# A linear-attention block and a ternary feed-forward on one Trainium2 core: the last block's output in two halves, and 32 row matmuls in three pieces

## What is computed

```python
q, k, v = x@Wq.T + bq, x@Wk.T + bk, x@Wv.T + bv        # 16 heads of 16 channels
q = softmax(q, axis=-1); k = softmax(k, axis=-2)        # k over the tokens
state = einsum('bhnd,bhne->bhde', k, v)
out   = einsum('bhnd,bhde->bhne', q, state)
x = layernorm(x + (layernorm(out)*ln_g + ln_b) @ Wo.T + bo)
h = layernorm(x)*ln1_g + ln1_b
h = gelu(h @ ternary(w1).T + b1)                        # 256 -> 1024
y = (layernorm(h)*ln2_g + ln2_b) @ ternary(w2).T + b2   # 1024 -> 256
x = layernorm(x + y)
```

## Time and profile before

| what | value |
|---|---|
| median of 3 runs | 592.26 us (591.04 to 594.32) |
| profiled execution, its own time | 591.67 us |
| its span, first to last instruction | 589.9 us |
| mean granted TensorE clock | 0.985 |
| busy share: PE, DVE, ACT, POOL | 93%, 86%, 82%, 68% |
| chain that ended last, by engine | PE 56%, POOL 14%, ACT 11%, DVE 10%, issue 5%, DMA 2% |

### The profile page before, as it was taken

How to read it: one execution, slowest core, us unless ns; L and a number is a source line. 1 busy time by engine, 2 the same in 40 slices (tenths; PEclk the granted TensorE clock), 3 DMA queues, 4 the chain that set the end, 5 groups by cost and what they waited for, 6 DMA issues and landing times.

```text
span 589.9 us, 10943 instructions
## 1 busy us (share of the span) xinstructions
PE 549.4 (93%) x3584; PEld 498.6 (85%) x3584; DVE 507.2 (86%) x1294; ACT 480.8 (82%) x938; POOL 398.3 (68%) x384
## 2 busy tenths in 40 slices
PE   1989999999999999999699999999999999999990
PEld 1879999999889999988679888888988888889890
DVE  3998888787979878866767999999999999999985
ACT  4461779787868978775979999999999999999983
POOL 0463779769597876658647876667678766765672
PEclk9999999999999999989999999999999999999996
DMA  5632013060613203052010022211212222010002
GB/s 161 266 118 73 1 73 144 0 215 2 221 66 134 83 11 135 1 181 107 37 71 2 2 107 73 72 36 38 73 72 73 71 75 66 34 45 37 37 37 107
DMA packets 11256, 46.53 MB, mean 79 GB/s; under 512 B 1344, under 2 KB 1728, under 8 KB 9024
## 3 DMA queue, kind: packets, MB, share of 16 engines
q1 hardware_dynamic: 11200, 45.83, 21.6%
HBM read 29.02 MB, written 16.81 MB: 78 GB/s over the span
## 4 chain that ended last, share of the span: by engine, by line
PE 56%; POOL 14%; ACT 11%; DVE 10%; issue 5%; DMA 2%; POOLq 0%; SPq 0%; ACTq 0%; DVEq 0%
PE ring L1727 18%; PE qps_sps_aps_then_y L1751 18%; PE qps_sps_aps_then_y L1600 5%; PE qps_sps_aps_then_y L1617 4%; POOL xt L401 3%; POOL xc_lo L380 3%; POOL xt_lo L390 3%; ACT z L677 2%; ACT zjunk L669 2%; PE ring L1540 2%; PE qps_sps_aps_then_y L1522 2%; PE ring L1669 2%; POOL qw L411 2%; DVE z L1092 1%; ACT ring L720 1%
## 5 line engine op out<-in xcount | busy, mean ns | idle before, releaser
L1751 PE MATMUL qps_sps_aps_then_y<-ff_w_over_xc_lo,ff_a_lo_over_qw 128*128 128x258 f32 x512 | 126.3, 283 | 0.0
L1751 PE MATMUL qps_sps_aps_then_y<-ff_w_over_xc_lo,ff_a_hi_over_xc_lo 128*128 128x258 f32 x512 | 126.2, 283 | 0.0
L1727 PE MATMUL ring<-ff_ht_hi_over_qw,t 128*128 128x512 f32 x256 | 106.1, 414 | 3.0 <-DVE ff_sums L1218 1.1
L1727 PE MATMUL ring<-ff_ht_lo_over_xc_hi,t 128*128 128x512 f32 x256 | 101.2, 395 | 0.0
L1751 PEld LDWEIGHTS qps_sps_aps_then_y<-ff_w_over_xc_lo,ff_a_hi_over_xc_lo 128*128 128x128 f32 x512 | 96.9, 189 | 3.5
L1751 PEld LDWEIGHTS qps_sps_aps_then_y<-ff_w_over_xc_lo,ff_a_lo_over_qw 128*128 128x128 f32 x512 | 96.6, 189 | 3.4
L1179 DVE SCALAR_TENSOR_TENSOR ff_a_lo_over_qw<-ring,ff_rho,ff_a_hi_over_xc_lo 128x512 fp32r<-128x512 f32 x128 | 91.5, 741 | 7.9 <-ACT ff_a_hi_over_xc_lo L738 6.9
L720 ACT ACTIVATE ring<-ring,bias 128x512 f32<-128x512 f32 x128 | 84.1, 675 | 11.8 <-PE ring L1727 10.5
L493 POOL TENSOR_TENSOR ff_accp_over_xt_lo<-ff_accp_over_xt_lo,ff_sq_over_ek_et_hi 128x512 f32<-128x512 f32 x64 | 84.0, 1313 | 11.4 <-ACT ff_sq_over_ek_et_hi L736 7.0
L736 ACT ACTIVATE ff_sq_over_ek_et_hi<-ring 128x512 f32<-128x512 f32 x128 | 78.7, 615 | 0.5
L738 ACT CAST ff_a_hi_over_xc_lo<-ring 128x512 fp32r<-128x512 f32 x128 | 77.5, 605 | 0.0
(11 more groups left out here) (175 smaller groups left out, 1673.0 us busy)
## 6 DMA issues: line engine op xcount, KB each, us to landing
x_scratch<-z SPq DMA_DIRECT2D x16, 514.0 KB, 3.0
ff_x_over_w_raw_xc<-x_scratch SPq DMA_DIRECT2D x16, 514.0 KB, 4.7
xt<-in_x_tok_dram SPq DMA_DIRECT2D x8, 1024.0 KB, 4.8
out_dram<-ff_z_over_et_lo SPq DMA_DIRECT2D x16, 512.0 KB, 3.5
xc<-in_x_chan_dram SPq DMA_DIRECT2D x7, 1024.0 KB, 6.9
w_raw<-in_w_dram SPq DMA_DIRECT2D x2, 1024.0 KB, 6.5
xc<-in_x_chan_dram SPq DMA_DIRECT2D x2, 512.0 KB, 6.8
rows<-in_rows_dram SPq DMA_DIRECT2D x1, 384.0 KB, 6.5
```

What stands on the lines that cost most here:

```text
L1727: mm = nc.tensor.matmul(ff_bank(k, m), t1[:, c, m * P:(m + 1) * P], h[:, k % 2, c], start=(c == 0 and j == 0), stop=(c == CH - 1 and j == 1))
L1751: last = nc.tensor.matmul(ff_yps[:, t, 0:C + 2], a[:, m % DEPTH, t * P:(t + 1) * P], ff_w2[:, m], start=(m == 0 and j == 0), stop=(m == FC ...
```

## The change

Three edits.

1. `ternary_rows` takes a range. 8 of the 32 matmuls stay at their place, 16 go between `state_product(7)` and `state_transpose(7)`, 8 between `state_transpose(7)` and `ff_first(0,0)`. `folded_rows` moves in DVE's list from before `k_maximum(7,1)` to behind `projected_low(7)`, and POOL's `ff_keep_residual(0, .)` gets a wait for it (`f_out` at 3).
2. On DVE `ff_hidden_stats(15)`, which leads to the block's first variance (the hidden one), goes ahead of `ff_centre_y(15, .)`. The last iterations of DVE's loop are written out.
3. Block 15 gets small tiles of its own (`l_mv`, `l_ve`, `l_rs`, `l_shift`) and goes in halves of two token tiles: variance, power, shift for each half. ACT scales tiles 0, 1 and 2, DVE tile 3, and SP stores two halves of 256 KB.

```diff
 (SP)
             ff_store(NK - 2)
-            ff_store(NK - 1)
-            for par in range(2):
-                sp.wait_ge(ff_o_out[par], 8 * NK)
+            for g in range(2):
+                sp.wait_ge(l_act, g + 2)
+                if g == 1:
+                    sp.wait_ge(l_dve, 1)
+                sp.dma_start(out[NB - 1, :, T - TB + 2 * g:T - TB + 2 * g + 2], ff_z[:, (NK - 1) % 2, 2 * g:2 * g + 2]
+                             ).then_inc(ff_o_out[(NK - 1) % 2], 16)
+            sp.wait_ge(ff_o_out[0], 8 * NK)
+            sp.wait_ge(ff_o_out[1], 8 * NK + 16)
 (POOL, ff_keep_residual and the end of its list)
                 if k == 0:
                     pool.wait_ge(xe_mm, NB)
+                    pool.wait_ge(f_out, 3)
...
-            for k in range(4, NK + 4):
+            for k in range(4, NK + 3):
...
+            for g in range(2):
+                pool.wait_ge(l_eps, g + 1)
+                nc.gpsimd.tensor_tensor(l_rs[:, 2 * g:2 * g + 2], l_ve[:, 2 * g:2 * g + 2], nhalf[:, 0:2], ALU.pow
+                                        ).then_inc(l_rstd, 1)
 (ACT)
-            for k in range(3, NK + 3):
+            for k in range(3, NK + 2):
...
+            for n in range(3):
+                act.wait_ge(l_nmr, n // 2 + 1)
+                nc.scalar.activation(ff_z[:, (NK - 1) % 2, n], ff_z[:, (NK - 1) % 2, n], ACT.Identity,
+                                     bias=l_shift[:, n:n + 1], scale=l_rs[:, n:n + 1]).then_inc(l_act, 1)
 (DVE)
+            def last_variance(g):
+                ts = slice(2 * g, 2 * g + 2)
+                dve.wait_ge(ff_z_stat, TB * (NK - 1) + 2 * g + 2)
+                nc.vector.memset(fence[:], 0.0)
+                for n in range(2 * g, 2 * g + 2):
+                    nc.vector.bn_aggr(l_mv[:, n], ff_bnZ[:, n]).then_inc(ff_z_var, 1)
+                dve.wait_ge(ff_z_var, TB * (NK - 1) + 2 * g + 2)
+                nc.vector.tensor_scalar(l_ve[:, ts], l_mv[:, ts, 1], EPS, None, ALU.add).then_inc(l_eps, 1)
+
+            def last_shift(g):
+                ts = slice(2 * g, 2 * g + 2)
+                dve.wait_ge(l_rstd, g + 1)
+                nc.vector.scalar_tensor_tensor(out=l_shift[:, ts], in0=l_mv[:, ts, 0], scalar=-1.0, in1=l_rs[:, ts],
+                                               op0=ALU.mult, op1=ALU.mult).then_inc(l_nmr, 1)
...
-            folded_rows()
             k_maximum(NB - 1, 1)
...
             projected_low(NB - 1)
+            folded_rows()
             product_stats(NB - 1, 0)
...
+            ff_residual(NK - 2, (2, 3))
+            ff_hidden_mean(NK - 1)
+            ff_hidden_stats(NK - 1)
+            ff_centre_y(NK - 1, (0, 1))
+            ff_centre_y(NK - 1, (2, 3))
+            ff_out_stats(NK - 2, (2, 3))
+            ff_out_variance(NK - 2)
+            ff_residual_gain(NK - 1)
+            ff_residual(NK - 1, (0, 1))
+            ff_out_stats(NK - 1, (0, 1))
+            ff_out_shift(NK - 2)
+            last_variance(0)
+            ff_residual(NK - 1, (2, 3))
+            ff_out_stats(NK - 1, (2, 3))
+            last_variance(1)
+            last_shift(0)
+            last_shift(1)
+            dve.wait_ge(l_nmr, 2)
+            nc.vector.tensor_scalar(ff_z[:, (NK - 1) % 2, 3], ff_z[:, (NK - 1) % 2, 3], l_rs[:, 3:4], l_shift[:, 3:4],
+                                    ALU.mult, ALU.add).then_inc(l_dve, 1)
 (PE)
-            def ternary_rows():
-                pe.wait_ge(f_tern, 8)
-                pe.wait_ge(f_bsum, 1)
...
+            def ternary_rows(first, last):
+                if first == 0:
+                    pe.wait_ge(f_tern, 8)
+                    pe.wait_ge(f_bsum, 1)
+                for n in range(first, last):
...
-            ternary_rows()
+            ternary_rows(0, 4)
             attend(NB - 2, 0)
...
             state_product(NB - 1)
+            ternary_rows(4, 12)
             state_transpose(NB - 1)
+            ternary_rows(12, 16)
             ff_first(0, 0)
             state_project(NB - 1)
```

More of the change, by code:

```diff
@@ L165, in both_halves @@
         ff_gain = sb("ff_gain", [P, TB])
+        l_ve, l_rs, l_shift = sb("l_ve", [P, TB]), sb("l_rs", [P, TB]), sb("l_shift", [P, TB])
+        l_mv = sb("l_mv", [P, TB, 2])
         early = ExitStack()
@@ L250, in both_halves @@
             sem(s) for s in ("ff_yc_ok", "ff_z_ok", "ff_z_stat", "ff_z_var", "ff_z_eps", "ff_z_rstd", "ff_z_nmr", "ff_o_ok"))
+        l_eps, l_rstd, l_nmr, l_act, l_dve = (sem(s) for s in ("l_eps", "l_rstd", "l_nmr", "l_act", "l_dve"))
         ff_o_out = [sem(f"ff_o_out{n}") for n in range(2)]
@@ L1432, in _ @@
             ff_hidden_stats(0)
-            for k in range(1, NK + 2):
+            for k in range(1, NK - 1):
                 ff_norm_apply(k + 2, (0, 1))
@@ L1458, in _ @@
                 ff_hidden_stats(k)
+            ff_out_stats(NK - 3, (2, 3))
+            ff_act_low(NK - 1, 3)
+            ff_act_low(NK - 1, 4)
+            ff_out_variance(NK - 3)
+            ff_residual_gain(NK - 2)
+            ff_act_low(NK - 1, 5)
+            ff_residual(NK - 2, (0, 1))
+            ff_out_stats(NK - 2, (0, 1))
+            ff_act_low(NK - 1, 6)
+            ff_act_low(NK - 1, 7)
+            ff_square_sum(NK - 1, 7)
+            ff_out_shift(NK - 3)
+            ff_square_total(NK - 1)
+            ff_residual(NK - 2, (2, 3))
[18 more added lines that the diff above has]
+                                    ALU.mult, ALU.add).then_inc(l_dve, 1)
         @block.tensor
@@ L1490, in ternary_bias @@
                 last.then_inc(f_bias, 1)
-            def ternary_rows():
-                pe.wait_ge(f_tern, 8)
-                pe.wait_ge(f_bsum, 1)
[L1495 to L1503, removed]
+            def ternary_rows(first, last):
[3 more added lines that the diff above has]
+                for n in range(first, last):
+                    h, m = n // FC, n % FC
+                    for piece in range(2):
+                        j = VEC[("ln2_g", "ln2_b")[h]][0] + m
+                        mm = nc.tensor.matmul(
+                            qps[:, h * C:(h + 1) * C], vparts[:, j, piece:piece + 1].to_broadcast([P, P]),
+                            t2[:, m], start=(n == 0 and piece == 0),
+                            stop=(m == FC - 1 and piece == 1), skip_group_check=True)
+                if last == 2 * FC:
+                    mm.then_inc(f_rows, 1)
             def q_product(b, v):
```

## The result

The changed kernel takes **586.74 us** (median of 4 runs, 586.42 to 587.22); the kernel before took 591.95 us beside it (4 runs, 591.04 to 594.32). The ratio is 0.989, with a 95% interval of 0.987 to 0.991: 5.2 us faster. The forecast was 585.4 us.

The account below looks back on a forecast made before the run. PE bounds the feed-forward blocks, row matmuls the path near 261 us, a serial tail the end. Terms -4.0 - 0.65 - 0.7 - 0.9 - 0.6 = -6.9 us: profiled 584.8, forecast 585.4 against median 592.26; range 583.4 to 588.3.

Parts of the forecast that it names:

- First place, -4.0: Around 261 us, 24 of 32 row matmuls leave (3.04 us) and PE's 0.99 us wait goes: -4.0 us, other end 2.5.
- POOL's lateness: At the change of stage, POOL's ff_rs late by some 0.5 us, absorbed; rival that POOL limits the gain to 2.5: chance 0.11.
- Second place, 0: Change of stage: 2.9 us of moved matmuls meet 4.0 us of PE idle time, so 0 us.
- Clock -0.65: state_project(7): filled PE gaps keep the clock at its upper level, 1.66 us becomes 1.01: -0.65 us, ends 0 and 0.65.
- port -0.7: r_lo of batch 7: a new wait holds POOL's ff_x1c behind it, 1.69 us becomes 0.96: -0.7 us, ends 0 and 0.73.
- End, scalings -0.9: Last block in halves: tile 2 scaled at 585.8 to 585.9 instead of 586.79, -0.9 us including +0.2 for hidden variance first.
- Store -0.6: Last store: the last 256 KB needs half of the 1.28 us transfer of 512 KB, -0.6 us, ends 0 and half of 1.28.
- the forecast's own sign of being wrong: At the end: a last store that lands 2.6 us after issue would show the forecast wrong; 2.0 us would show it right.
- the working beside it: Last store: by the skill's DMA fit, fixed part about 2.0 us, a half saves 0.3 us and the sum is smaller by 0.3.
- Feed-forward 0: Feed-forward stage, attend(7,0) to PE's last transposes: no change, 0 us, blocks still 16.9 us.
- the port as a rival: At the end: first half's power on POOL beside DVE's residual, one waits, up to 1.0 us lost, 586.4; chance 0.05.
- Attention stage, 0: Start to state_project(6), which holds nothing of the change: forecast difference 0 us.

Follow-up runs that it names:

- first filler: Kernel before plus 24 matmuls whose result nothing reads, in PE's gaps, first of two runs; state_project(7) to attend(7,0) 3.81 us, before 5.20.
- The clock alone: Kernel before, all 32 row matmuls in place, plus 24 unread matmuls in PE's gaps at the change of stage; timed ratio 0.998 (0.9954 to 0.9998).
- the port alone: Kernel before plus one wait, POOL's ff_x1c of block 0 until r_lo of batch 7 is done; state_project(7) to attend(7,0) 5.71 us.
- the run with the new end alone: Kernel before with only edits 2 and 3 (hidden variance ahead of centring, last block in two halves with two stores); ratio 1.000 (0.999 to 1.002).
- the control: The changed kernel itself once more, beside a run with its costly parts undone; 586.56 us (586.37 to 588.73), ratio to before 0.991.

## Why the prediction was right, and where it wasn't

By its own terms:

- **First place, -4.0: right.** From `state_project(6)` to the end of `ff_transposes(0, .)` 3.8 us went. It depends on the clock: where it fell near 260 us both with and without the change (before and after), it is 3.8 us; where it fell in neither (first filler and edit 1 alone), 3.04. A fall cost 1.1 us there while all 32 rows stood in the place, and 0.3 us after the change, when PE had 0.98 us of waiting for `r_lo` that hid the rest (the row of the kernel with edit 1 alone). So some 0.8 of the 3.8 us hung on the fall, which the forecast did not have as a condition. POOL's lateness cost PE nothing (0.28 us, expected 0.5).
- **Second place, 0: right**, +0.15 us measured.
- **Clock -0.65 and port -0.7: the sum was right (-1.40), the division wrong.** The step that failed is the one that took the two as separate causes that add. The clock alone gives all 1.40 us, the port alone nothing where the clock was low to the end. The forecast read `r_lo`'s 1.69 us as POOL's doing, which it is, but didn't ask why `r_lo` came second to the port: because PE's slow `state_project(7)` had made it late. The new wait for `f_out` was not needed for this gain (`ff_x1c` needs it all the same, since it reads `ff_c_row`).
- **End, scalings -0.9: right in sign, too small.** -1.22 us, although edit 2 cost 0.31 and not 0.2. The mis-sized term was the power of POOL: 1.01 us was taken for each, and on two columns it took 0.86 and 0.70. The second is the one on the path; of its 0.31 us some 0.1 is not had, because ACT is still at tile 1 when the second shift is ready.
- **Store -0.6: wrong**, +0.26 us. The step was "the last 256 KB needs half of that". The two stores overlap, the second half is issued 0.5 us behind the first, so 512 KB still have to move behind a point only half a microsecond earlier; the last half landed 2.9 us after its issue, and the forecast's own sign of being wrong was 2.6. The rule to coalesce was the better guide, but the working beside it was not right: DMA: Bandwidth & Descriptors (Anatomy of one DMA) of the Trainium skill gives that fit for the GpSimd path, and these stores go over SP's queue. As an estimate by the fit's slope (bytes / 436e3) 512 KB takes 1.2 us to move, close to the 1.28 us of the earlier trace rows, and a half would save 0.6 us and not 0.3. What disagrees with the fit is the total, 3.2 us by it against 2.6.
- **Feed-forward 0: wrong**, +0.44 us, 0.39 of it 23.2 us behind `attend(7,0)`, by the timelines from the port of POOL and DVE. The forecast had the port as a rival, but at the end, where it cost nothing (`ff_z` 0.87 us beside the power). It did not look for other meetings of the two engines that a shift of some tenths could turn round.
- **Attention stage, 0**: +0.47 us between the two profiles, and scatter.

For the profiled execution the forecast was 584.8 us and it took 586.55. The difference of 1.75 us is the store (0.88), the first stretch (0.47), the feed-forward stage (0.44) and the change of stage (0.28), less the scalings (0.32). None of the rivals occurred as written; the port of POOL and DVE did cost time, but at another place than the rival had it.

## What to carry to other kernels

Two prices at one place in a chain need not add: ask of each whether it is still there once the other is gone, and whether it is the cause or the effect. Idle time of PE ahead of a critical stretch can cost more than it lasts, through the granted clock, and moved work (even useless work) that fills it is worth more than its own hiding. When a change shifts engines against each other, look along the rest of the timeline for pairs of instructions of DVE and POOL that both read SBUF and start within some tenths of each other. A split of the last transfer gains nothing while its first part is still under way when the second is issued; no run here shows a split that pays.

## What was not expected of the hardware

- **Who starts first keeps the port.** `z` took 0.48 us when it began 0.11 us ahead of `ff_x1c`, 1.50 when it began 0.22 us behind; `r_lo` 0.96 and 1.69. SBUF — State Buffer (Who interferes with whom) of the Trainium skill has this rule, that issue order decides who blocks, for a DVE instruction with two SBUF inputs, and the trace agrees. What tips the contest isn't shown: `ff_rs` ahead of it took 1.30 to 1.32 us in the seven profiles where no loss came (it began 0.03 to 0.05 us behind the first `z`), and 1.01 to 1.03 in the seven others, where it began 0.02 to 0.04 us behind, among them the run with the new end alone, whose lists up to there are those of before.
- **POOL's power is not such a holder.** Its 0.86 us beside the last residual left both `ff_z` at 0.87 us together, as when alone. The same section of the Trainium skill has the loser held for the whole instruction; there the trace differs.
- **A fall of the clock comes in some executions and not in others.** Over the 14 profiles it came near 39 us in seven, near 169 us in three and near 260 us in eleven. Those with the one near 169 us reached `state_project(6)` at 259.40 to 259.92 us, all others at 256.59 to 258.83. So part of the scatter of a time seems to be the number of falls in it: the control's two runs at a mean clock of 0.983 took 588.7 us, its others, at 0.988 and more, 586.4 to 586.6.
